# Turning x1 on VectorE instead of TensorE, and the slots that this moves, in a decoder layer kernel

## The reference

```
x = layernorm(x + self_attention(x))                  # 3 iterations
x = layernorm(x + cross_attention(x, ctx))            # q = x Wq, k = ctx Wk, v = ctx Wv, softmax(q k / 4) v, Wo
x = layernorm(x + ffn(x))                             # base x W_base, plus one of 8 adapters, chosen per batch
                                                      # by the least reconstruction loss of 8 encoder/decoder pairs
```

## Time and profile before

| | |
|---|---|
| median of 3 runs | 1651.06 us (1650.19 to 1655.74) |
| the profiled execution | 1650.58 us, its span 1648.8 us, mean granted clock 0.989 |
| TensorE busy | 1586.7 us, 96% |
| VectorE busy | 1238.2 us, 75% |
| ScalarE busy | 1053.2 us, 64% |
| GpSimd busy | 161.2 us, 10% |

### The profile page before, as it was taken

The page is one execution under the profiler, slowest core; times in us unless marked ns, Lnnn a source line. Parts: engine busy times, 40 slices in busy tenths (PEclk is TensorE's granted clock), DMA queues, the critical chain, the costliest instruction groups (busy, mean ns, idle before and its releaser), DMA issues.

```text
span 1648.8 us, 25559 instructions
## 1 busy us (share of the span) xinstructions
PE 1586.7 (96%) x9632; PEld 588.7 (36%) x9632; DVE 1238.2 (75%) x1790; ACT 1053.2 (64%) x1998; POOL 161.2 (10%) x151
## 2 busy tenths in 40 slices
PE   6779999999999999999999999999999999999997
PEld 5442323332333333332333323433333323332233
DVE  5788777877788777887888777887778777887522
ACT  2227776676666666676666766676666776666661
POOL 7311000100011000100001000110001000000000
PEclk8899999999999999999999999999999999999999
DMA  5655071623517071442707163361707234150010
GB/s 156 116 143 101 25 138 41 101 69 86 96 40 127 28 131 40 90 93 62 116 22 134 32 113 69 69 112 52 121 12 122 61 52 77 50 78 5 11 33 16
DMA packets 118663, 125.22 MB, mean 76 GB/s; under 512 B 35186, under 2 KB 100339, under 8 KB 118540
## 3 DMA queue, kind: packets, MB, share of 16 engines
q1 hardware_dynamic: 117724, 123.06, 38.3%
q10 hardware_dynamic: 816, 0.53, 0.1%
HBM read 84.18 MB, written 35.03 MB: 72 GB/s over the span
## 4 chain that ended last, share of the span: by engine, by line
PE 85%; DVE 7%; ACT 3%; issue 3%; DMA 1%; SPq 0%; POOL 0%; POOLq 0%; DVEq 0%; ACTq 0%
PE banks L1122 23%; PE values L1141 23%; PE banks L1082 12%; PE work L1012 5%; PE work L998 5%; PE work L957 4%; DVE xneg_max_pieces L1439 4%; PE work L1019 3%; PE work L1025 3%; ACT xprobs L1260 3%; PE work L1004 2%; PE work L1028 1%; PE work L942 1%; PE work L1037 1%; DMA max_dram<-xneg_max_rows 1%
## 5 line engine op out<-in xcount | busy, mean ns | idle before, releaser
L1260 ACT ACTIVATE xprobs<-banks 128x512 f32<-128x512 f32 x1664 | 900.5, 595 | 408.3 <-PE banks L1122 405.0
L1439 DVE TENSOR_REDUCE xneg_max_pieces<-banks 128x2 f32<-128x1024 f32 x768 | 909.0, 1219 | 258.4 <-PE banks L1082 257.2
L1122 PE MATMUL banks<-xq_stacks,xk_stacks 99*128 99x512 bf16 (+1 forms) x1664 | 517.7, 385 | 9.9 <-ACT xprobs L1260 3.0
L1141 PE MATMUL values<-xprobs,xv_rows 128*17 128x512 f32 x3328 | 437.9, 598 | 1.3 <-ACT xprobs L1260 1.3
L1122 PEld LDWEIGHTS banks<-xq_stacks,xk_stacks 99*128 99x128 bf16 (+1 forms) x1664 | 127.4, 97 | 398.8 <-ACT xprobs L1260 273.2
L1082 PE MATMUL banks<-xk_stacks,xq_stacks 49*128 49x512 bf16 (+1 forms) x2048 | 250.3, 335 | 14.2 <-DVE xneg_max_pieces L1439 12.3
L1082 PEld LDWEIGHTS banks<-xk_stacks,xq_stacks 49*128 49x128 bf16 x2048 | 57.2, 94 | 327.6 <-DVE xneg_max_pieces L1439 212.9
L1510 POOL TENSOR_TENSOR xk_parts<-xk_rest,xk_parts 128x401 bf16<-128x401 f32 (+1 forms) x64 | 59.0, 923 | 660.5 <-ACT xk_parts L1239 660.5
L1141 PEld LDWEIGHTS values<-xprobs,xv_rows 128*17 128x17 f32 x3328 | 55.1, 95 | 122.9 <-issue 117.6
L1505 POOL TENSOR_TENSOR xrstd<-xrstd,mhalf 128x4 f32<-128x4 f32 x23 | 23.2, 1011 | 652.4 <-DVE xrstd L1314 652.4
L1012 PEld LDWEIGHTS work<-xvT,ctxT_a 128*128 128x128 f32 (+1 forms) x416 | 54.3, 192 | 13.6 <-issue 3.9
(11 more groups left out here) (295 smaller groups left out, 1007.3 us busy)
## 6 DMA issues: line engine op xcount, KB each, us to landing
xk_stacks<-key_parts_dram SPq DMA_DIRECT2D x186, 200.1 KB, 13.0
key_parts_dram<-xk_parts SPq DMA_DIRECT2D x144, 100.0 KB, 2.2
xq_stacks<-parts_dram SPq DMA_DIRECT2D x186, 64.0 KB, 8.8
ctxT_a<-in_ctxT SPq DMA_DIRECT2D x4, 1601.0 KB, 7.5
ctxT_b<-in_ctxT SPq DMA_DIRECT2D x4, 1601.0 KB, 7.5
parts_dram<-xq_parts SPq DMA_DIRECT2D x45, 128.0 KB, 2.0
key_parts_dram<-xk_parts SPq DMA_DIRECT2D x48, 100.2 KB, 5.2
xa<-in_x SPq DMA_DIRECT2D x8, 512.0 KB, 16.3
```

The costliest lines, as they stand in the source:

```text
L1122: pe.matmul(at, kst[0:ROWS[par], k, h2, par, t * P:(t + 1) * P], qst[0:ROWS[par], k, h2, par, :], start=True, stop=True).then_inc(made, 1)
L1141: last = pe.matmul(av[32 * j:32 * j + HD + 1, :], vals[:, k, t, gr * GH + j, :], probs[:, sl % 2, j, :], start=t == 0, stop=t == XKT - 1)
L1260: nc.scalar.activation(probs[:, sl % 2, j, :], score_bank(n)[0], ACT.Exp).then_inc(exped, 1)
L1439: nc.vector.tensor_reduce(nmp[:, of % 2, :, j2, q, piece], pairs[n % MRING][:, :, :], AX.X, ALU.max, negate=True).then_inc(on["mxr"], 1)
```

## The change

The transposes of x1 leave TensorE and ScalarE. VectorE does them with 16 transposes of 32 x 32 blocks (the step "turn"), each from 32 partitions of xa to 32 partitions of xT, 256 elements a partition, spread over slots 13 to 22. The query projection and the load of the next x wait for a new semaphore x1_turned. The slots' lists are written anew: v3 gets an end slot of its own (14), x2T 1 goes from slot 16 to 15, qproj 0 from slots 12 and 13 to 23 and 24, kproj 4 from slot 22 to 25, gram 2 is done in two slots instead of three, the loss goes from slot 35 to 34 and the adapter's choice with it. In slot 5 the scale step comes ahead of the two normalizing steps. On SP the query parts are stored after the max rows.

```diff
-        IN_BETWEEN = {
-            8: ("x1T", 0, NEXT), 11: ("x1T", 1, NEXT), 14: ("x2T", 0, PREV), 16: ("x2T", 1, PREV), 18: ("v", 3, NOW),
-            35: ("loss", 0, PREV),
-        }
+        IN_BETWEEN = {14: ("x2T", 0, PREV), 15: ("x2T", 1, PREV), 34: ("loss", 0, PREV)}
         SLOT_END = [
             (("kproj", 0, NEXT), 1), (("kproj", 1, NEXT), 1), (("v", 0, NOW), 2), (("v", 1, NOW), 2),
             (("xo", 0, PREV), 2), (("xo", 1, PREV), 2), (("kproj", 2, NEXT), 1), (("kproj", 3, NEXT), 1),
-            (("qproj", 0, NEXT), 2), (("v", 2, NOW), 2), (("enc", 0, PREV), 2), (("gram", 0, PREV), 2),
-            (("enc", 1, PREV), 2), (("kproj", 4, NEXT), 1), (("gram", 1, PREV), 2), (("enc", 2, PREV), 2),
-            (("gram", 2, PREV), 3), (("enc", 3, PREV), 2), (("gram", 3, PREV), 2), (("kproj", 5, NEXT), 1),
+            (("v", 2, NOW), 2), (("v", 3, NOW), 1), (("enc", 0, PREV), 2), (("gram", 0, PREV), 2),
+            (("enc", 1, PREV), 2), (("gram", 1, PREV), 2), (("qproj", 0, NEXT), 2), (("kproj", 4, NEXT), 1),
+            (("enc", 2, PREV), 2), (("gram", 2, PREV), 2), (("enc", 3, PREV), 2), (("gram", 3, PREV), 2),
...
         VECTOR_WORK = {
-            14: [("invert", "o", 0, NOW)], 18: [("scale", "o", 0, NOW)],
+            13: turn_steps(0, 1), 14: [("invert", "o", 0, NOW), *turn_steps(1, 2)], 15: turn_steps(2, 3),
+            16: turn_steps(3, 5), 17: turn_steps(5, 7), 18: [("scale", "o", 0, NOW), *turn_steps(7, 8)],
+            19: turn_steps(8, 9), 20: turn_steps(9, 11), 21: turn_steps(11, 14), 22: turn_steps(14, N_TURNS),
...
-            5: [*norm_steps("apply", "x1", 0, 2, NEXT), ("scale", "o", 3, PREV)],
+            5: [("scale", "o", 3, PREV), *norm_steps("apply", "x1", 0, 2, NEXT)],
...
             elif name == "qproj":
                 if part == 0 and not ph.first:
-                    pe.wait_ge(on["w_free"], ph.order.after(("x1T", 1, b)))
+                    pe.wait_ge(x1_turned, N_TURNS * b)
...
+            elif name == "turn":
+                a, c = divmod(q, P // 32)
+                if q == 0:
+                    v.wait_ge(on["normed"]["x1"], b)
+                v.transpose(xT[32 * c:32 * (c + 1), :, :].rearrange("p k (n a i) -> p a k n i", a=P // 32, i=32)[:, a],
+                            xa[32 * a:32 * (a + 1), :, :].rearrange("p n (k c i) -> p c k n i", k=CH, i=32)[:, c]
+                            ).then_inc(x1_turned, 1)
...
             sp_move_outputs(m)
-            if nxt < B:
-                sp_query_parts(0, uses_before(0, nxt))
             sp_spread_inverses(m)
             sp_max_rows(m + 2)
             if nxt < B:
+                sp_query_parts(0, uses_before(0, nxt))
                 sp_free_key_dram(nxt, 1)
                 sp_key_parts(4, use + 4)
```

More of the change, by code:

```diff
@@ L789, in cross_attention_and_ffn @@
         scaled = sem("x_outputs_scaled")
+        x1_turned = sem("x_x1_turned")
         x1_in = sem("x_x1_in")
@@ L838, in cross_attention_and_ffn @@
             (("xo", 0, PREV), 2), (("xo", 1, PREV), 2), (("kproj", 2, NEXT), 1), (("kproj", 3, NEXT), 1),
-            (("qproj", 0, NEXT), 2), (("v", 2, NOW), 2), (("enc", 0, PREV), 2), (("gram", 0, PREV), 2),
-            (("enc", 1, PREV), 2), (("kproj", 4, NEXT), 1), (("gram", 1, PREV), 2), (("enc", 2, PREV), 2),
-            (("gram", 2, PREV), 3), (("enc", 3, PREV), 2), (("gram", 3, PREV), 2), (("kproj", 5, NEXT), 1),
-            (("kproj", 6, NEXT), 1), (("kproj", 7, NEXT), 1), (("v", 4, NEXT), 2), (("v", 5, NEXT), 2),
-            (("mid", 0, PREV), 2), (("y", 0, PREV), 2), (("y", 1, PREV), 2), (("v", 6, NEXT), 2),
+            (("v", 2, NOW), 2), (("v", 3, NOW), 1), (("enc", 0, PREV), 2), (("gram", 0, PREV), 2),
+            (("enc", 1, PREV), 2), (("gram", 1, PREV), 2), (("qproj", 0, NEXT), 2), (("kproj", 4, NEXT), 1),
+            (("enc", 2, PREV), 2), (("gram", 2, PREV), 2), (("enc", 3, PREV), 2), (("gram", 3, PREV), 2),
+            (("kproj", 5, NEXT), 1), (("kproj", 6, NEXT), 1), (("kproj", 7, NEXT), 1), (("v", 4, NEXT), 2),
+            (("v", 5, NEXT), 2), (("mid", 0, PREV), 2), (("y", 0, PREV), 2), (("y", 1, PREV), 2), (("v", 6, NEXT), 2),
             (("qproj", 1, NEXT), 2), (("v", 7, NEXT), 1),
@@ L854, in norm_steps, with turn_steps @@
             return [(step, what, q, rel) for q in range(first, last)]
+        N_TURNS = (P // 32) ** 2
+        def turn_steps(first, last):
+            return [("turn", "x1", n, NEXT) for n in range(first, last)]
         def choose_steps(first, last):
@@ L868, in cross_attention_and_ffn @@
             11: norm_steps("apply", "x2", 0, 2, PREV), 12: norm_steps("apply", "x2", 2, 4, PREV),
-            35: choose_steps(0, 4), 36: choose_steps(4, 8), 37: choose_steps(8, CHOOSE_STEPS),
+            34: choose_steps(0, 4), 35: choose_steps(4, 8), 36: choose_steps(8, CHOOSE_STEPS),
             45: norm_steps("stats", "y", 0, 2, PREV), 47: norm_steps("stats", "y", 2, 4, PREV),
@@ L1545, in sp_load_x @@
                 nc.sync.wait_ge(on["x1_out"], 16 * (b - 1))
-                nc.sync.wait_ge(on["w_free"], MAIN.order.after(("x1T", 1, b - 1)))
+                nc.sync.wait_ge(x1_turned, N_TURNS * (b - 1))
             nc.sync.dma_start(xa[:], g.x[b].rearrange("(q p) d -> p q d", p=P)).then_inc(on["x_in"], 16)
```

## The result

The changed kernel takes 1678.01 us (median, 1676.05 to 1679.57); the kernel before, on the same chip, 1650.67. The ratio is 1.0158, with an interval of 1.0135 to 1.0181: slower by 1.6%, where 0.5% was forecast. The profiled execution took 1676.05 us, its span is 1674.2.

The account below looks back on a forecast made before the run. TensorE was taken as the bound, busy 188.35 of 189.06 us a batch. Against 1650.58 us, -10.2 - 2.4 + 1.4 + 0.6 = -10.6, with +18.6 for SP's queue, made +8.0: 1658.6 us, range 1640 to 1668.

Parts of the forecast that it names:

- Transposes off TensorE: Slots 8 and 11 lose the x1 transposes, 0.57 + 0.89 us in each of 7 batches: -10.2 us.
- Scale before apply: The x2 product of slot 6 no longer waits for VectorE's scaling, 0.4 us in 6 batches: -2.4 us.
- 16 turns: VectorE's turns in slots 13 to 22 take 440 ns each; the last make slot 23 wait: +1.4 us.
- bounds of 212 and 690: Limits in ns for one turn on VectorE: 212 gives no wait, 690 costs +2.3 us a batch.
- the rival with slow turns: Turns at 0.69 us with moves held: 1672 us, chance 0.10; with moves not held 1653, chance 0.03.
- The hold weighed in the prediction: Each VectorE turn might lose 0.08 us of overlap by output partition group, making the sum 2.4 us higher.
- Slots rearranged: New places for v3, x2's second half and gram 2 cost 0.1 us in each of 6 batches: +0.6 us.
- The queue on SP: Group 1's moves wait behind the context load, blocking VectorE 5.1 us, in batches 0 to 5: +18.6 us.
- 3.1 us lost: TensorE's second pair of slot 29, due at V26 + 11.3, starts at 14.4; counted in six batches.
- Right behind it in the queue: SP issues the moves just after the context load, so they cannot land before it, V26 + 11.0.
- Moves not held: Rival: small transfers slip past the context load and land by V26 + 8.3: 1640.0 us, chance 0.19.
- Held, but shorter: Rival: context load faster than 7.3 us or TensorE's loss under 1.8 us a batch: 1646 to 1651, chance 0.08.

Follow-up runs that it names:

- kernel 4: Kernel 1 with x1 transposed by TensorE again in slots 8 and 11 and no turns on VectorE: 1656.51 us, ratio 1.0024.
- kernel 5: The kernel before, with only the scale step put ahead of the x1 normalizing steps in slot 5: 1651.66 us, ratio 1.0009.
- Kernel 7: Kernel 1 with each of the 16 turns done twice into the same place, the second waiting for the first: 1696.48 us, ratio 1.0284.
- kernel 1: The changed kernel with the context load issued on SP ahead of the query parts and key parts 4: 1646.61 us, ratio 0.9972.
- kernel 2: The changed kernel with 12 useless products on TensorE ahead of the pairs in slot 29 of batches 1 to 5: 1663.38 us, ratio 1.0073.
- kernel 9: The changed kernel with the context load issued by ScalarE into its own DMA queue, behind the first exponential of slot 27: 1672.81 us, ratio 1.0143.
- kernel 8: The changed kernel with the context load issued by ScalarE into its own DMA queue, behind the mid part of key projection 4: 1652.14 us, ratio 0.9997.
- kernel 6: The changed kernel with the moves of group 1's outputs ahead of key parts 4 and the context load on SP: 1666.78 us, ratio 1.0109.

## Why the prediction was wrong, step by step

*Transposes off TensorE*, forecast -10.2: right, 11.9 by kernel 4. There slot 8 gives 0.90, not 0.57, in batches 1 to 6.

*Scale before apply*, forecast -2.4: alone, in the old order, it is wrong in size and gives 0.7 (kernel 5), since slots 7 and 8 take back 0.42 of the 0.51 of slot 6. But the 0.25 of slot 8 is a wait of the transposes, and they are gone in the changed kernel. So these two terms can't be parted cleanly: counted from the kernel before, slot 8 gives 0.66, the transposes 10.5 and the scale 2.0 (six times 0.51 - 0.17), both near their forecasts. Their sum is 12.6 either way, within 0.1.

*16 turns*, forecast 440 ns and +1.4 of waits: 436 ns, and 0.03 us in slot 23, +0.2. The bounds of 212 and 690 and the rival with slow turns are out. The hold weighed in the prediction has a row now: three turns take 1.37 us (0.47 from start to start), while two reductions of 1.22 take 2.36; it cost no time here. Kernel 7 says how near the edge it was: once, the 7 us are hidden; twice, 5.0 us of the second 7.5 show in the batch that keeps its clock, and up to 7.7 where the clock falls too.

*Slots rearranged*, forecast +0.6. By slots of kernel 1 in a middle batch: 14 to 16 +0.03, 18 to 20 -0.58, 22 to 25 +0.04, 26 +0.08, 29 +0.79, 34 and 35 +0.04, together +0.4, so +2.4. These four give -11.9 - 0.7 + 0.2 + 2.4 = -10.0 in place of -10.6. Kernel 1's span is 8.2 below that of before; its median is only 4.7 below, and two batches have a slot 12 that waits 1.2 and 1.35 us more. What spreads its runs over 10 us is open.

*The queue on SP.* In batch 3 the clockwork came true to a fifth of a microsecond: load issued at V26+3.50 (3.7), moves in at 12.39 (12.2), wait of 5.13 (5.1), TensorE going again at 14.38 (14.4). **The step that failed is the price put on it: "3.1 us lost", six times, +18.6.** Slot 29 has 5.8, 5.8, 4.7, 6.0 and 4.6 too much in batches 1 to 5, and slots 29 and 30 of batch 0 have 5.3 together: 32.2 us. Two things were missing. The larger is the clock. The step counted TensorE's work behind the wait at full speed, but TensorE comes back at 1.2 GHz. Kernel 2 parts the two for batches 1 to 5: 3.3 us a batch of wait, close to the forecast, and 2.1 of clock. In batch 0 some 1.7 of the 5.3 are the clock (an estimate from its granted clock of 0.88 and 0.77 in slots 29 and 30). That makes 12 us of clock, which the sum put at nothing, and 20 of wait for its 18.6. The smaller: the load lands 7.7 to 9.3 us after its issue in batches 1 to 5, not 7.3, so batches 1 and 4 wait longer than batch 3. Check: -10.0 + 32.2 + 1.7 in the part ahead of slot 1 + 1.7 in slot 12 of batches 5 to 7 = +25.6; the span grew by 25.4.

The reason given for that step was half right. "Right behind it in the queue" isn't what holds the moves (kernel 9); that they are in flight beside it is. The evidence of the earlier trace rows could not tell the two apart, for there too both transfers stood in one queue.

*The rivals.* "Moves not held" does not happen by itself; kernel 1 brings it about, and gets 1646.6 by median where 1640.0 was worked out. *Held, but shorter* has its like in kernel 8, 1652.1, where the load goes out 2.4 us earlier.

## What to carry to other kernels

When an edit moves the work that a transfer waits for, look at what will be in flight beside it: here the small transfers that met a 1.6 MB load were in only 8 to 11 us after its issue, up to 6 us late, from either of the two queues tried, and moving the victim only picked the next one (kernel 6). The cure was to move the load to a stretch where nothing small was held up (kernel 1: 0.28% faster than before, interval 0.12 to 0.44%, from a change that was 1.6% slower). A wait on a TensorE that is full has two prices, the idle time and the clock behind it; and time won by letting one engine ask sooner is given back where it next waits for the engine that answers (kernel 5), unless that wait goes too.

## What the runs showed of the hardware

- In batch 3 TensorE had 2.4 GHz all through slots 26 to 28 of the changed kernel (granted clock 1.00), had little to do for some 4 us in slot 29 (busy 1.45 of 4.17 us, at full clock), and then ran at 1.2 GHz for most of the next 4.20 us. By the windows above the lower level lasts (1 - 0.83) / 0.5 x 10.02 = 3.4 us in batch 1 and (1 - 0.67) / 0.5 x 9.97 = 6.6 in batch 2. The windows over the idle time and what follows it in batch 3:

```profile
794.43:798.60 4.17, 1.45 (x12) 0.23 (x12) 1.99 (x4) 0.98 (x2) 0.00 (x0) 1.00 0.54 92
798.60:802.80 4.20, 4.20 (x9) 1.73 (x10) 2.20 (x2) 1.09 (x2) 0.00 (x0) 0.59 0.63 124
```

- Twelve useless products in that gap kept the granted clock at 1.00 and saved 10.3 us in slot 29 of five batches (kernel 2).
- Small transfers in flight with a 1601 KB load waited for nearly all of it even from another queue: their waiter started 8.7 to 9.2 us after the load's issue in batches 1 to 5 of kernel 9, and no packet of theirs had started when 165 packets of the load had gone in the stretch shown.
- A turn of 32 x 256 elements of 4 bytes takes 436 ns on VectorE, and the next one starts 0.47 us after it.
